# A graph network on one core: dense products written out block by block, and packed window numbers for the filling of tiles

## What is computed

```python
Q = relu(x @ query_kernel + query_bias)[row]      # layer 0: attention
K = relu(x @ key_kernel + key_bias)[col]
V = (x @ kernel)[col]
e = (x_dst - x_src) @ theta_w.T + x_src @ phi_w.T # layer 1: edges
h = x @ W                                         # layer 2: convolution
h = relu(out @ W1 + b1)                           # layer 3: two dense layers
return h @ W2 + b2
```

## Time and profile before

| | us |
|---|---|
| median of 3 runs | 11548.42 (11541.08 to 11550.59) |
| the profiled execution's own time | 11562.99 |
| its span | 11561.4 |
| the fill's stretch | 828.0 |
| the dense phases qk, v, pr, h | 53.3, 41.3, 44.6, 40.6 |
| the dense phases m1, m2 | 52.1 each |

### The profile page before, as it was taken

How to read it: one execution, slowest core, us unless ns; L and a number is a source line. 1 busy time by engine, 2 the same in 40 slices (tenths; PEclk the granted TensorE clock), 3 DMA queues, 4 the chain that set the end, 5 groups by cost and what they waited for, 6 DMA issues and landing times. The chain is left out here.

```text
span 11561.4 us, 331562 instructions
## 1 busy us (share of the span) xinstructions
PE 8920.2 (77%) x101102; PEld 7210.5 (62%) x101103; DVE 8515.2 (74%) x17511; ACT 4614.1 (40%) x9076; POOL 1655.6 (14%) x2115
## 2 busy tenths in 40 slices
PE   6144557885888755899994888798899959849996
PEld 5132224664777644899993655433899946649995
DVE  7497777777999866666666666666788867788887
ACT  0021001112666411566663333476677746613332
POOL 0010000110000000466661000000000003301110
PEclk9999999998999855999997999899999979979996
DMA  1100000000444311333333999677455510000000
GB/s 37 13 0 11 4 4 8 11 11 12 168 165 165 124 36 31 112 123 125 125 123 103 320 313 322 229 250 237 131 144 144 144 40 5 5 3 3 3 3 12
DMA packets 617056, 1103.62 MB, mean 95 GB/s; under 512 B 119640, under 2 KB 207539, under 8 KB 616992
## 3 DMA queue, kind: packets, MB, share of 16 engines
q1 hardware_dynamic: 487488, 923.21, 25.3%
q10 hardware_dynamic: 121152, 168.86, 3.9%
q0 software_dynamic: 8352, 10.85, 0.4%
HBM read 901.57 MB, written 201.10 MB: 95 GB/s over the span
## 5 line engine op out<-in xcount | busy, mean ns | idle before, releaser
L2439 POOL TENSOR_TENSOR acc<-acc,m_sum 128x544 f32<-128x544 f32 (+1 forms) x637 | 816.2, 1281 | 1237.5 <-ACT m_sum L2406 953.6
L2369 PE MATMUL m_sps<-m_msg,m_oh 128*128 128x136 f32 x5096 | 722.5, 286 | 0.0
L2304 DVE TENSOR_TENSOR m_msg<-m_vps,m_msg 128x512 f32<-128x512 f32 x637 | 440.7, 692 | 361.4 <-PE m_vps L2345 269.9
L2558 DVE BATCH_NORM_STATS2 stats<-t_es 128x512 f32 x637 | 442.2, 694 | 353.0 <-ACT t_es L2591 351.6
L2759 PE MATMUL u_sps<-u_r,u_oh 128*128 128x128 f32 x5096 | 678.1, 276 | 28.7 <-ACT u_r L2717 28.7
L2570 PE MATMUL t_eps<-t_oht,p_parts 128*128 128x512 bf16 x1911 | 527.9, 386 | 211.8 <-DVE t_oht L1472 208.3
L2743 PE MATMUL u_zps<-fcs,u_a 128*128 128x128 f32 x5112 | 677.5, 276 | 7.3 <-ACT u_a L2711 7.3
L2644 PE MATMUL g_z<-g_a,fcT 128*128 128x512 f32 x1274 | 616.2, 616 | 66.2 <-ACT g_a L2633 54.4
L1408 PE MATMUL sp_out_x<-x,sp_adj_x 128*128 128x128 f32 x4802 | 661.8, 281 | 0.0
L1392 PE MATMUL sp_aps_x<-sp_ohw_x,sp_oh_x 128*128 128x128 bf16 x7644 | 545.2, 219 | 146.6 <-DVE sp_ohw_x L1359 146.6
L1421 ACT COPY sp_adj_x<-sp_aps_x 128x512 f32<-128x512 f32 x637 | 373.4, 586 | 702.4 <-PE sp_aps_x L1392 702.4
(11 more groups left out here) (584 smaller groups left out, 21493.9 us busy)
## 6 DMA issues: line engine op xcount, KB each, us to landing
u_e<-e_tiles SPq DMA_DIRECT2D x640, 256.0 KB, 2.8
e_tiles<-t_es ACTq DMA_DIRECT2D x637, 256.0 KB, 5.6
g_e<-e_tiles SPq DMA_DIRECT2D x637, 256.0 KB, 3.5
s_rows<-bucket_rows SPq DMA_DIRECT2D x148, 768.0 KB, 4.0
m_rows<-bucket_rows SPq DMA_DIRECT2D x148, 768.0 KB, 4.1
t_rows<-bucket_rows SPq DMA_DIRECT2D x148, 768.0 KB, 7.1
s_rows<-bucket_rows SPq DMA_DIRECT2D x49, 1024.0 KB, 5.3
m_rows<-bucket_rows SPq DMA_DIRECT2D x49, 1024.0 KB, 5.3
```

The lines of the kernel that those rows point to most:

```text
L2369: last = nc.tensor.matmul(sps[x][:, at:at + M], oh[x][:, j * P:(j + 1) * P], msg[x][:, j * M:(j + 1) * M], start=True, stop=True)
L2439: nc.gpsimd.tensor_tensor(at, at, sums[x][:, 0:n * M], ALU.add).then_inc(added, 1)
```

## The change

**Packed numbers.** The tables phase computes one more kind of number for each window, `wspan`: the block, plus 64 times its first group, plus 32768 times the first group of the next block. `span` loads `wspan` and the offset, and takes the three numbers out of it with shifts and masks. SP writes one more row with a DMA and waits for it as well.

**Dense products.** The loop is gone: all 50 blocks are written out, so every address is fixed, and PE turns a block straight from the table. There are three buffers of each kind instead of two, and one semaphore of a kind instead of two. PE turns two blocks ahead of the one that it multiplies. DVE evacuates block b and then adds the bias to block b - 1.

```diff
@@ phase_bucket_tables
+                c.step(nc.vector.memset(spans[:, :], 0.0))
+                c.step(nc.vector.tensor_scalar(spans[:, 0:s.NB], L["gstart"][:, 1:s.NB + 1], 32768.0, None, ALU.mult))
+                c.step(nc.vector.scalar_tensor_tensor(out=spans[:, 0:s.NB], in0=L["gstart"][:, 0:s.NB], scalar=64.0, in1=spans[:, 0:s.NB],
+                                                      op0=ALU.mult, op1=ALU.add))
+                c.step(nc.vector.tensor_tensor(spans[:, 0:s.NB], spans[:, 0:s.NB], k["iota_f"][:, 0:s.NB], ALU.add))
+                c.go(nc.vector.tensor_copy(T["wspan"][:, 0:s.NB], spans[0:1, 0:s.NB]))
+                for t, v in zip(got, (k["iota_f"], xst, L["gcount"], adj, spans)):
                     c.step(nc.vector.tensor_tensor(x3(e2), x3(e1), v[:, 0:NB1].unsqueeze(1).broadcast_to([P, XC, NB1]), ALU.mult))
                     c.step(nc.vector.tensor_reduce(t[:, :], x3(e2), AX, ALU.add))
                 c.step(nc.vector.memset(tab[:, :], 0.0))
                 c.go(nc.vector.tensor_copy(tab[:, 0:XC], got[0][:, :]))
+                c.go(nc.vector.tensor_copy(tab[:, 16:16 + XC], got[4][:, :]))
...
+                sp.dma_start(T["wspan"][:, s.NB:], ti[16:16 + XC, :]).then_inc(row_io, 16)
                 sp.dma_start(T["wcoff"][:, s.NB:], ti[32:32 + XC, :]).then_inc(row_io, 16)
                 sp.dma_start(rows[0:1, :].rearrange("o (c x) -> (o c) x", x=P), tf[0:XC, :]).then_inc(row_io, 16)
-                sp.wait_ge(row_io, 48)
+                sp.wait_ge(row_io, 64)
                 sp.dma_start(T["wkey"][:, s.NB:], rows[0:1, :].broadcast_to([P, B.XW])).then_inc(row_io, 16)
-                sp.wait_ge(row_io, 64)
+                sp.wait_ge(row_io, 80)
@@ phase_bucket_fill, span
-            b = B.block(eng, s, w)
-            g0 = eng.value_load(L["grow"][0:1, bass.ds(b, 1)], min_val=0, max_val=z.NGS - 1)
-            g1 = eng.value_load(L["grow"][0:1, bass.ds(b + 1, 1)], min_val=1, max_val=z.NGS)
+            packed = eng.value_load(T["wspan"][0:1, bass.ds(w, 1)], min_val=0, max_val=(1 << 24) - 1)
+            b = (packed & 63).with_bounds(min_val=0, max_val=s.NB - 1)
+            g0 = ((packed >> 6) & 511).with_bounds(min_val=0, max_val=z.NGS - 1)
+            g1 = (packed >> 15).with_bounds(min_val=1, max_val=z.NGS)
             off = eng.value_load(T["wcoff"][0:1, bass.ds(w, 1)], min_val=0, max_val=1 << 20)
@@ phase_dense
-    F = weights.shape[1]
-    with ExitStack() as ctx:
-        sb, ps, sem = scope(nc, ctx, k)
-        xb = [sb(f"d_xb{u}" + tag, D) for u in range(2)]
-        xT = [sb(f"d_xT{u}" + tag, D) for u in range(2)]
-        tps = [ps(f"d_tps{u}" + tag, P) for u in range(2)]
-        ops = [ps(f"d_ops{u}" + tag, F) for u in range(2)]
-        sums = [sb(f"d_sum{u}" + tag, F) for u in range(2)] if bias is not None else ops
-        S = {n: [sem(f"d_{n}{u}") for u in range(2)] for n in ("copied", "turned", "xT_ready", "product", "biased", "evacuated")}
-        n = s.NB1 // 2
+    F, R = weights.shape[1], 3
+    with ExitStack() as ctx:
+        sb, ps, sem = scope(nc, ctx, k)
+        xT = [sb(f"d_xT{u}" + tag, D) for u in range(R)]
+        tps = [ps(f"d_tps{u}" + tag, P) for u in range(R)]
+        ops = [ps(f"d_ops{u}" + tag, F) for u in range(R)]
+        sums = [sb(f"d_sum{u}" + tag, F) for u in range(R)] if bias is not None else ops
+        turned, xT_ready, product, biased, evacuated = (sem("d_" + x) for x in ("turned", "xT_ready", "product", "biased", "evacuated"))
+        n = s.NB1
         with nc.Block() as block:
             @block.vector
             def _(dve):
-                for u in range(2):
-                    dve.sem_inc(S["turned"][u], 1)
-                    dve.sem_inc(S["product"][u], 1)
-
-                def take(i):
-                    for u in range(2):
-                        dve.wait_ge(S["turned"][u], i)
-                        nc.vector.tensor_copy(xb[u][:, :], src[:, bass.ds(((i - 1) * 2 + u) * D, D)]).then_inc(S["copied"][u], 1)
-
-                def turn(i):
-                    for u in range(2):
-                        dve.wait_ge(S["turned"][u], i + 1)
-                        dve.wait_ge(S["product"][u], i)
-                        nc.vector.tensor_copy(xT[u][:, :], tps[u][:, :]).then_inc(S["xT_ready"][u], 1)
-
-                def add_bias(i):
-                    for u in range(2):
-                        if bias is not None:
-                            dve.wait_ge(S["product"][u], i + 1)
-                            dve.wait_ge(S["evacuated"][u], i)
-                            nc.vector.tensor_tensor(sums[u][:, :], ops[u][:, :], bias[:, :], ALU.add).then_inc(S["biased"][u], 1)
-                take(1)
-                with dve.Fori(1, n) as i:
-                    turn(i)
-                    take(i + 1)
-                    add_bias(i)
-                turn(n)
-                add_bias(n)
+                def add_bias(b):
+                    dve.wait_ge(product, b + 1)
+                    if b >= R:
+                        dve.wait_ge(evacuated, b - R + 1)
+                    nc.vector.tensor_tensor(sums[b % R][:, :], ops[b % R][:, :], bias[:, :], ALU.add).then_inc(biased, 1)
+                for b in range(n):
+                    dve.wait_ge(turned, b + 1)
+                    if b >= R:
+                        dve.wait_ge(product, b - R + 1)
+                    nc.vector.tensor_copy(xT[b % R][:, :], tps[b % R][:, :]).then_inc(xT_ready, 1)
+                    if bias is not None and b:
+                        add_bias(b - 1)
+                if bias is not None:
+                    add_bias(n - 1)
 
             @block.tensor
             def _(pe):
-                with pe.Fori(1, n + 1) as i:
-                    for u in range(2):
-                        pe.wait_ge(S["copied"][u], i)
-                        nc.tensor.transpose(tps[u][:, :], xb[u][:, :], k["ident"][:, :]).then_inc(S["turned"][u], 1)
-                    for u in range(2):
-                        pe.wait_ge(S["xT_ready"][u], i)
-                        if bias is None:
-                            pe.wait_ge(S["evacuated"][u], i)
-                        nc.tensor.matmul(ops[u][:, :], xT[u][:, :], weights[:, :], start=True, stop=True).then_inc(S["product"][u], 1)
+                def turn(b):
+                    if b >= R:
+                        pe.wait_ge(xT_ready, b - R + 1)
+                    nc.tensor.transpose(tps[b % R][:, :], src[:, b * D:(b + 1) * D], k["ident"][:, :]).then_inc(turned, 1)
+                turn(0)
+                turn(1)
+                for b in range(n):
+                    if b + 2 < n:
+                        turn(b + 2)
+                    pe.wait_ge(xT_ready, b + 1)
+                    if b >= R:
+                        pe.wait_ge(evacuated if bias is None else biased, b - R + 1)
+                    nc.tensor.matmul(ops[b % R][:, :], xT[b % R][:, :], weights[:, :], start=True, stop=True).then_inc(product, 1)
 
             @block.scalar
             def _(act):
-                for u in range(2):
-                    act.sem_inc(S["evacuated"][u], 1)
-                with act.Fori(1, n + 1) as i:
-                    for u in range(2):
-                        if bias is None:
-                            act.wait_ge(S["product"][u], i + 1)
-                        else:
-                            act.wait_ge(S["biased"][u], i)
-                        for c0, c1, func, dest in outs:
-                            last = nc.scalar.activation(dest((i - 1) * 2 + u), sums[u][:, c0:c1], func)
-                        last.then_inc(S["evacuated"][u], 1)
+                for b in range(n):
+                    act.wait_ge(product if bias is None else biased, b + 1)
+                    for c0, c1, func, dest in outs:
+                        last = nc.scalar.activation(dest(b), sums[b % R][:, c0:c1], func)
+                    last.then_inc(evacuated, 1)
@@ gnn_kernel, and likewise at the other calls of phase_dense
-                    phase_dense(nc, s, k, k["x"], w[:, :], None, [(0, D, ACT.Copy, lambda b: vf[:, bass.ds(b * D, D)])], "_v")
+                    phase_dense(nc, s, k, k["x"], w[:, :], None, [(0, D, ACT.Copy, lambda b: vf[:, b * D:(b + 1) * D])], "_v")
```

More of the change, by code:

```diff
@@ L824, in __init__ @@
         self.WM = s.NB + self.XW
+        assert self.XC <= 16 and z.NGS <= 511 and s.NB < 64
         def sb(name, cols, dt=F32, parts=P):
@@ L1042, in phase_bucket_tables @@
         e1, e2 = sb("bt_e1", XC * NB1), sb("bt_e2", XC * NB1)
-        got = [sb(f"bt_got{n}", XC) for n in range(4)]
+        got = [sb(f"bt_got{n}", XC) for n in range(5)]
+        spans = sb("bt_spans", NB1)
         tab, fl = sb("bt_tab", 96), sb("bt_fl", 2, F32, 1)
@@ L3377, in gnn_kernel @@
                 phase_dense(nc, s, k, k["x"], w[:, :], None,
-                            [(0, D, ACT.Copy, lambda b: pf[:, bass.ds(b * D, D)]),
-                             (D, 2 * D, ACT.Copy, lambda b: rf[:, bass.ds(b * D, D)])], "_pr")
```

(2 more changed lines are left out.)

13 lines of the change are left out of this document (6 added, 7 removed).

## The result

The changed kernel takes 11369.19 us (median of 4 runs, 11361.03 to 11383.33), the kernel before 11544.75 us on the same chip (median of 4, 11535.7 to 11550.59): a ratio of 0.985, interval 0.9838 to 0.9863, and 175.6 us less. The profiled execution took 11361.03 us with a span of 11359.5. On a second chip the same program gave 0.9841 (0.9826 to 0.9855, 11331.94 against 11521.84 us). The forecast was 11398 us, in a range of 11368 to 11450: the measured time lies 1.2 us inside the range's lower end.

What follows compares the result with a forecast made beforehand. Phases between barriers add up: DVE's side ends the fill's borders, and PE waits in each dense pair. Gains of 64 (fill) and 89.5 us (dense), less 3.6 (tables), make 150 us: 11398 us, range 11368 to 11450.

Steps and rivals of the forecast that it cites:

- the chain through DVE: Dense phases with a bias: DVE's order sets the step at 2.4 GHz, 0.76 us a block in qk, 0.56 in m.
- the gain of the fill: Fill: 49 borders, each 1.3 us shorter, give 64 us (51 to 74).
- the 1.5 us for two loads: Fill's border: two of four loads go on both engines, saving 1.5 us a border.
- The unpacking: Fill's border: three register instructions on DVE replace the loads and cost 0.2 us, between 0 and 0.45.
- The trips: Fill's inner loop: upper bounds worked out anew 439 times on DVE and PE, costed at 0, at most 13 us.
- PE's pitch: Dense phases: PE's stream sets 0.76 us a 128-column block at 1.2 GHz, 0.44 at 2.4; 256 columns 1.08 or 0.64.
- Time at 1.2 GHz: Dense phases: each stays slow for 8 us, the shortest shown before (pr), then runs at 2.4 GHz.
- Entries and ends: Dense phases' entries: idle time may change by -0.5 to +2.1 us each, taken as 0, up to 13 us for the range.
- The clock as before: Rival, 24%: dense phases' clock rises when it did before, in m never; gain 119 us, 11429 us.
- The border held elsewhere: Rival, 8%: PE or the loops' bounds give back half the fill's gain; 11430 us, up to 11460.
- The fill's clock: Rival, 4%: PE's clock rises in the fill, 75 us more gained, 11323 us.
- Code that comes too slowly: Rival, 3%: written-out dense phases wait for code, 14 waits a phase at 2.1 us, 11575 us.

Runs made afterwards that it cites:

- second profile: The kernel before run once more, unchanged, to profile it again; 11511.53 us.
- spare turns: Kernel before with two spare PE turns in each pair of every dense phase, 11484.15 us; or with 29 ahead of qk's loop, 11564.26 us.

## Why the prediction was right, and where it was not

**Direction and mechanism** held: the loads left the border, the turning ahead made PE's stream dense, the clock rose in m, and the chain through DVE set the step where there is a bias. The sizes were less good than the total looks. The measured gain, 175.6 us, lies 26 above the forecast of 150. By phases the change gave 56.3 - 3.7 + 122.3 = 175 us, and the 11 of scores and maxima besides; the forecast was 64 - 3.6 + 89.5. So the gain of the fill was forecast 8 too high and that of the dense phases 33 too low, which partly cancel, and 11 us came from phases that no term covers. That the time fell inside the range, by 1.2 us, is luck: by the second chip's ratio of 0.9841 it would be 0.9841 x 11548.4 = 11365 us, 3 below the range. The 122 us, like the forecast, are measured from the first profile of before; from its second profile they are 106.

**Fill.** The term that was off is the 1.5 us for two loads. Two steps go from the first load to the third, which the page prints at 1068.3 and 1069.8; in the trace's nanoseconds it is 1.42, and the time ahead of `bf_cur` fell by 1.41. The unpacking was taken at 0.2 and took 0.22, though not where I looked for it. A border got 1.19 us shorter instead of 1.3, which is 5.3 us over 49. The trips, taken at 0, cost 390 x 0.0044 = 1.7. DVE was to be idle for 1.4 us ahead of `bf_cur` and is for 1.27, as the unpacking went behind it. The Trainium skill, DMA: Bandwidth & Descriptors, in its measured facts, has 600 ns as the floor of a load; the row shows 0.30, and two steps gave 1.41 with their checks, which would be 2.0 by the page's figure. The measurement decides.

**Tables.** The packing was forecast at 3.6 us and took 3.7.

**PE's pitch** was the largest error. I took (0.71 - 0.275)/3 = 0.145 us a pass from four passes in one row, and 0.27 from another. The four belong to two products, and the second had to wait for its block: the single starts in that row are 0.21, 0.11 and 0.11 apart, and 0.38, 0.21, 0.21 in the slow one. The passes that wait for nothing are the true pitch, 0.11 and 0.21. The two turns in the earlier trace rows were 0.22 apart, and half of that, at twice the clock, is 0.11: the number was there. At 1.2 GHz too a block is 0.64 us and not 0.76. A block in v and h is 0.33 and not 0.44, over 39.5 blocks 4.2 us in each; in pr 0.543 and not 0.64, 4.1 us.

**The chain through DVE** held, and was sized within 8%: 0.706 where 0.76 was forecast in qk, 0.535 where 0.56 was in m. Putting the bias later removed it. At 1.2 GHz it was said to stay under PE's stream; in m it did not quite, as blocks came 0.64 and 0.74 us apart there by turns, where PE's passes take 0.64.

**Time at 1.2 GHz** was taken as 8 us a phase and was 3.6 to 5.8. The early rise was in the range's lower end only. What I weighed as against it, that v was idle for little and stayed slow for 26 us, does not carry over: with turns ahead PE is busy for 19.1 of v's 20 us, and it was for 35.3 of 41.3 before, the largest share of any dense phase there.

**Entries and ends** were taken as 0. From phase to phase the six gave 122.3 us, by their own work (first turn to last activation) 284.0 - 166.5 = 117.5: 5 us, 0.8 each, are ends and entries. In m2 the first turn comes 1.2 us after m1's last activation, where the first copy came 1.7 after it.

**The rivals.** The clock as before (24%) fell, since it rose in m. The border held elsewhere (8%) fell too: the trips gave back 1.7 us, not 32. The fill's clock (4%) did not rise. Code that comes too slowly (3%) fell: pr's pitch is 0.543 us in every tenth of the phase between the first and the last, and v shows one wait of DVE that cost 0.3 us, where the rival wanted 14 a phase at 2.1 us. The code is fetched, though: the page of the profile counts 29 and 51 packets in the two instruction queues, where before has 21 and 43. The Trainium skill, Runtime: NRT & Kernel Launch, Instruction fetch mechanics, has straight code fetched ahead, and this agrees.

## What to carry to other kernels

Where PE's steps are short and its stream has gaps, an order that turns ahead can pay twice, once for the gaps and once for the clock. Here the writing out alone gave 47 us by one run, 15 of them in the scores and maxima, and written out with three buffers but with nothing turned ahead the kernel lost. A phase that stands at the edge of the clock has to be profiled more than once, before and after. Take the pitch of an engine from starts that follow each other without a wait, and see whether it halves with the clock. A loaded number costs its check too, here 0.28 us a load on a path that sets the end.

## What the runs showed of the chip

- The clock of the kernel before stood at an edge: m2, with identical code, took 52.1 us at 1.2 GHz in one profile and 41.4 us in another.
- More work made a phase faster: m1 took 40.4 us with 200 passes, and 52.1 with 150 in each of four profiles.
- The check of bounds of a loaded number takes 0.28 us of DVE's sequencer at a border (190 ns, 23 ns and the gaps), nearly what the load of 0.30 takes.
- Two phases with unchanged instructions were together 10 to 15 us shorter in every kernel with packed numbers or with written-out phases, and not in those that only had spare turns; why is open.
- The column of the granted clock reads 1.00 ahead of the first record of a trace, whatever the products show.
